# Sorting graph nodes on one core: destination blocks counted ahead of the weights, and row tiles mixed with the rank products

## What is computed

```python
edge_index = jnp.stack([src, dst])
x = x + _L0_gnn_ref(_layernorm(x), W, a_src, a_dst, edge_W, edge_b, bias, edge_attr_3, edge_index)
x = x + _L0_ffn_ref(_layernorm(x)[None], ...)[0]
x = x + _L1_gnn_ref(_layernorm(x), W_u, b_u, W_v, src, dst)
x = x + _L1_ffn_ref(_layernorm(x)[None], ...)[0]

# inside _L0_gnn_ref
h = (x @ W.T).reshape(n, H, D)
alpha = einsum(h[src], a_src) + einsum(h[dst], a_dst) + sum(enc * h[dst])   # then a softmax over each dst
out = jax.ops.segment_sum(h[src] * attn[..., None], dst, num_segments=n)
```

## Time and profile before

| | us |
|---|---|
| median of 3 runs | 4083.69 (4081.59 to 4086.49) |
| profiled execution, total | 4077.23 |
| its span | 4075.5 |
| sort stage, start to DVE's last operation | about 226 |
| last gather issued | 123.8 |
| ranks start on PE | 143.3 |
| placing starts on PE | 197.8 |

### The profile page before, as it was taken

One profiled execution on the slowest core, in us unless ns is written; L12 is line 12 of the kernel. 1 busy time (PEld: TensorE's weight loads), 2 busy tenths in 40 slices (PEclk: granted clock), 3 DMA queues, 4 the chain that ended last, 5 costly groups with the idle time before them and its releaser, 6 DMA issues. The chain is left out here.

```text
span 4075.5 us, 69197 instructions
## 1 busy us (share of the span) xinstructions
PE 2987.4 (73%) x12787; PEld 2165.0 (53%) x12788; DVE 2290.8 (56%) x5023; ACT 1295.0 (32%) x5485; POOL 2294.7 (56%) x2343
## 2 busy tenths in 40 slices
PE   4624777788888877989666656566665489999998
PEld 3422444444444444658544444444444388888887
DVE  4534888888888887864355555555555611111111
ACT  1402444444444444432211111111111533333333
POOL 5156777677777772002577777777777523333332
PEclk9857999899999998988777877877777799999999
DMA  8545444344444442000244444444444766665564
GB/s 185 152 92 131 114 115 113 100 106 105 105 105 105 108 108 53 0 2 32 78 112 113 113 113 113 113 112 113 113 113 112 216 186 168 166 170 165 170 174 123
DMA packets 284454, 477.32 MB, mean 117 GB/s; under 512 B 143854, under 2 KB 185660, under 8 KB 283892
## 3 DMA queue, kind: packets, MB, share of 16 engines
q0 software_dynamic: 127312, 321.61, 32.2%
q1 hardware_dynamic: 148203, 151.72, 12.7%
q10 hardware_dynamic: 8880, 3.34, 0.4%
HBM read 426.29 MB, written 50.68 MB: 117 GB/s over the span
## 5 line engine op out<-in xcount | busy, mean ns | idle before, releaser
L945 PE MATMUL g_pA<-g_msg,k_ident 128*128 128x264 f32 (+1 forms) x3712 | 1153.1, 464 | 475.5 <-DVE g_pA L1139 411.6
L945 PEld LDWEIGHTS g_pA<-g_msg,k_ident 128*128 128x128 f32 x3712 | 808.4, 229 | 808.7 <-issue 661.9
L900 POOL DMA_INDIRECT g_rows<-own,g_recs x928 | 879.4, 948 | 333.9 <-issue 262.8
L900 POOL DMA_INDIRECT g_rows<-rows,g_recs x928 | 879.6, 948 | 296.6 <-issue 194.7
L934 PE MATMUL g_pE<-g_ew,g_recT 128*128 128x512 f32 x932 | 515.4, 680 | 242.1 <-DVEq L1123 238.8
L1133 DVE TENSOR_TENSOR g_msg<-g_rows,g_pp 128x1024 f32 (+3 forms) x464 | 571.9, 1233 | 151.4 <-DVEq L84 151.3
L1983 POOL DMA_INDIRECT out<-e_ys,e_goal x102 | 160.6, 1575 | 505.8 <-issue 486.3
L934 PEld LDWEIGHTS g_pE<-g_ew,g_recT 128*128 128x128 f32 x932 | 171.4, 203 | 459.1 <-DVEq L1123 331.2
L2036 PE MATMUL e_pY<-e_w,e_hT 128*128 x1632 | 373.8, 382 | 35.5 <-issue 35.5
L1055 ACT ACTIVATE g_pp<-g_dd 128x32 f32<-128x32 f32 x464 | 95.2, 205 | 918.5 <-ACTq L84 918.5
L2025 PEld LDWEIGHTS e_pH<-e_xT,e_w 128*128 128x128 f32 x3264 | 381.6, 192 | 5.2
(11 more groups left out here) (419 smaller groups left out, 3533.5 us busy)
## 6 DMA issues: line engine op xcount, KB each, us to landing
e_w<-in_L_ffn_W SPq DMA_DIRECT2D x110, 1024.0 KB
g_rows<-own,g_recs POOLq DMA_INDIRECT x928
g_rows<-rows,g_recs POOLq DMA_INDIRECT x928
g_recs<-slots SPq DMA_DIRECT2D x468, 8.0 KB
tok<-e_xall SPq DMA_DIRECT2D x7, 910.0 KB
own<-p_row SPq DMA_DIRECT2D x50, 119.0 KB
p_x<-in_x SPq DMA_DIRECT2D x1, 5600.0 KB
own<-p_x SPq DMA_DIRECT2D x1, 5600.0 KB
```

What stands on the lines that cost most here:

```text
L900: pool.indirect_dma_start(out=rows[:, r, j, :], out_offset=None, in_=rows_d, in_offset=bass.IndirectOffsetOnAxis(ap=recs[:, r, 4 * j:4 * j ...
L945: last = t_.matmul(sums, K["ident"][:], of, start=False, stop=(j == C - 1), skip_group_check=True)
```

## The change

DVE's order is new: `index(0)` to `index(4)` and counts 0 to 19 first, then the record copies, counts 20 and 21, the weight preparation, and 50 statistics with a count after every third (counts 22 to 37); variance; count 38; scales; counts 39 to 49. On PE, 16 tiles come ahead of the ranks, two follow each of the seven rank steps, and 20 come last. POOL, ACT and SP keep their programs, UR = 3 included. `tiles` replaces `group`, and `ranks` becomes one step.

```diff
-        UR = 3
+        UR, EARLY = 3, 16
@@ VectorE
                 index(0)
-
+                index(1)
+                index(2)
+                for t in range(4):
+                    count(t)
+                index(3)
+                for t in range(4, 7):
+                    count(t)
+                index(4)
+                for t in range(7, 20):
+                    count(t)
+                dve.wait_ge(e_in, 64)
+                v.tensor_copy(rec[:, :, 0].bitcast(I32), srcw[:]).then_inc(rec_made, 1)
+                v.tensor_copy(rec[:, :, 1:4], attrw[:]).then_inc(rec_made, 1)
+                count(20)
+                count(21)
                 dve.wait_ge(w_in, 64)
...
                 dve.wait_ge(x_in, 32)
-                half = NT // 2
-                for t in range(half):
+                for t in range(NT):
                     norm.tile(v, t, x[:, t:t + 1, :])
-                for g in range(1, NT // GT):
-                    index(g)
-                for t in range(R):
-                    count(t)
-                for t in range(half, NT):
-                    norm.tile(v, t, x[:, t:t + 1, :])
+                    if t % 3 == 2:
+                        count(22 + t // 3)
                 ch.link(v.memset(norm.a[:], 0.0))
                 norm.variance(v, ch, stats)
-                dve.wait_ge(e_in, 64)
-                v.tensor_copy(rec[:, :, 0].bitcast(I32), srcw[:]).then_inc(rec_made, 1)
-                v.tensor_copy(rec[:, :, 1:4], attrw[:]).then_inc(rec_made, 1)
+                count(38)
                 dve.wait_ge(sq, 1)
                 norm.scales(v, ch, rst)
-                for t in range(R, NT):
+                for t in range(39, NT):
                     count(t)
@@ TensorE
-                def group(u, first, last_group):
-                    for r in range(W):
-                        if r < W - 1 or not last_group:
-                            turn(W * u + (r + 1), (r + 1) % 2)
-                        product(W * u + r, r % 2, first and r < 2)
+                def tiles(lo, hi):
+                    for t in range(lo, hi):
+                        if t + 1 < NT:
+                            turn(t + 1, (t + 1) % 2)
+                        product(t, t % 2, t < 2)
...
-                group(0, True, False)
-                group(1, False, False)
-                group(2, False, False)
-                ranks()
-                group(3, False, False)
-                group(4, False, True)
+                tiles(0, EARLY)
+                pe.wait_ge(hot_ok, 1)
+                for j in range(len(cols)):
+                    ranks(j)
+                    tiles(EARLY + 2 * j, EARLY + 2 * j + 2)
+                tiles(EARLY + 2 * len(cols), NT)
```

More of the change, by code:

```diff
@@ L536, in product, with ranks @@
                     last.then_inc(h_ok, 1)
-                def group(u, first, last_group):
-                    for r in range(W):
-                        if r < W - 1 or not last_group:
-                            turn(W * u + (r + 1), (r + 1) % 2)
-                        product(W * u + r, r % 2, first and r < 2)
[L544 to L552, removed]
+                def tiles(lo, hi):
[3 more added lines that the diff above has]
+                        product(t, t % 2, t < 2)
+                def ranks(j):
+                    a, b = cols[j]
+                    h = wide[:, a * NB:b * NB]
+                    w = (b - a) * NB
+                    if j:
+                        pe.wait_ge(taken, j)
+                    t_.matmul(pR[0:P, 0:w], K["tri"][0:P, 0:P], h, start=True, stop=True)
+                    t_.matmul(pTt[:, 0:w], K["ones"][0:P, 0:P], h, start=True, stop=True).then_inc(mm_ok, 1)
                 def place(g):
```

## The result

The changed kernel takes 4098.09 us (median; 4095.19 to 4100.98) where the kernel before takes 4083.15 beside it (4081.59 to 4086.49). The ratio is 1.0035, 95% interval 1.0023 to 1.0047: 14.9 us slower. 4090.5 was forecast, with a range up to 4097. Direction and mechanism were right; the loss is twice the forecast and 1 us beyond the range.

A forecast was written before the change was run, and what follows sets the result against it. The sort was taken as a chain hardly anything overlaps; the scan comes 14 earlier, but row tiles wait behind x's store, so placing starts 7.4 later, minus 0.6: +6.8, median 4090.5, range 4072 to 4097.

The forecast's parts named there:

- ACT's start: ACT's first row tile, after VectorE's counts and statistics: at 103.3 against 78.64, 24.7 later, with 1.3 added for slower landings.
- third rival: VectorE's statistics wait behind counts of late gathers: ACT up to 3.6 later, +10.4 in all, 4094; chance 0.12.
- catch up: VectorE's mixed loop, at 1.56 per count against POOL's 1.507, was said to recover from late gathers.
- PE's 16 tiles: TensorE's tiles ahead of the ranks: 25.2 from ACT's start, ending last, so ranks start at 128.5 against 143.25.
- The rank steps: TensorE's ranks mixed with tiles: 1.98 plus 2.5 for two tiles, period 4.5, 27.8 in all; scan at 156.9.
- x's issue: SP's store of x, still after row 29, now falls among row tiles: issued at 160.2, just as tiles 30 to 49 begin.
- Row 30's landing: Row 30's store, behind x in SP's queue and needed by row 35: lands 25 after 160.2, at 185.2; bounds 19 to 28.
- From there to placing: Fourteen tiles 18.6, low clock 2.2, minus 0.8: placing starts at 205.2, 7.4 later; tenth group 0.6 nearer.
- It costs nothing: SP's store of x in the kernel before, holding SP from 126.4 to 144.2 when no row tile runs, was priced at nothing.
- POOL: POOL's gathers: gather 13 leaves at 53.6, later ones every 1.507 without stall, the last at 107.9, 15.9 earlier.
- SP doesn't hold the tiles: Second x issue returns at once or row stores overtake x: placing 12.2 earlier, -12.8 in all, 4070.9; chance 0.14.
- short drain: Row 30 lands 19 after x's issue, the tail being mixed traffic's: +0.8, 4084.5; chance 0.14.

The follow-up runs named there:

- split runs: Changed kernel with x's 112 partitions stored after row 29 and its 13 after all rows: ratio 1.0016 to the kernel before; parts exchanged: 0.9990.
- x after row 39: Kernel before with UR = 4, so its store of x comes ten rows later: ratio 1.0030 to the kernel before, +13.3 us.

## Why the prediction was wrong in size

The sum to the placing was off by 6.3: +5.4 - 3.2 + 0.1 + 3.9 + 0.1.

- **ACT's start, +5.4: the failed step.** "Landings under it took up to 8.6 instead of 6.3; I add 1.3 (bounds 0 and 3.6)". One count waited 6.43 there, 5.1 more than that term. The statistics had begun 0.8 late (73.47 for 72.7), and the way from the last of them to ACT was 0.5 shorter, which makes the 5.4. The 8.6 was read from gathers issued from 80.07 on, when the record store had been in flight for two us and POOL had just paused. In the new order gathers are issued right at the store's start (71.75), and ten of them took 10.2 (median; up to 12.5). Moving the store away brought the landings back to 5.0 and removed the wait, so the cause is shown; that it is the first moments of the store that slow a gather most is my reading of two orders. It was the third rival's mechanism, and more than its 3.6: I gave it 0.12 as an alternative, and it came on top of my case. Nor did the loop "catch up", as I had it: from 82.53 on DVE has no pause in it (1.55 a round, as forecast), so it has no slack to make a wait good with.
- **PE's 16 tiles, 0.** Forecast 25.2 from ACT's start to the ranks; measured 133.93 - 108.70 = 25.2. The tiles ended last, as said.
- **The rank steps, -3.2.** Forecast period 4.5, measured 3.99 (133.93 to 137.92). I had 1.98 for the two rank products and 2.5 for two tiles, between PE's pace and ACT's. In the timeline they take 1.72 and 2.27; in the window PE is busy for all 3.99 and ACT for 2.42, so ACT no longer sets any of the pace.
- **x's issue, +0.1** from the scan (3.37 for 3.3). The step that the diff does not mention, and on which the forecast turned, was right: undoing it alone brings 20.6 us back (from +14.9 to -5.7).
- **Row 30's landing, +3.9: mis-sized.** Forecast 25 with bounds 19 and 28; measured 28.9, and 28.7 with `UR = 4`. I had the 27.2 of the drain from the row and went below it for the older traffic. The split runs show that the tail is x's own: the row store lies behind both parts, and the full drain is a lower bound, with the store's own time on top.
- **From there to placing,** 20.1 for 20.0, with two tiles at the granted clock of 0.53 (products of 2.03 and 1.70); the last group is 0.6 nearer, as said.
- **"It costs nothing"** of x's old place was wrong: DVE waited 7.16 for `following` beside it, and the ranks started about 6 later for it (x after row 39). It changed nothing in the sum, since the tiles ended last after the change (one-hot ready at 122.6, forecast 126.5).
- **POOL,** +2.3 on the last gather: gather 13 left at 54.87 instead of 53.6, and one issue took 2.09 instead of 1.20. The tiles hid it.

The rival that SP doesn't hold the tiles is refuted by the evictions. The short drain is too: it needed 19, and row 30 took 28.9, or 22.7 with the large part alone ahead of it. The range failed because its top put the bounds of my own case and the rival's delay side by side, not one on the other: the start's +5.4 and the landing's +3.9 make +9.3, and only the rank steps took 3.2 of it back. Each was beyond its own bound (+2.5 for the ranks' start, or 3.6 by the rival; 28 for the landing, which took 28.9). That the median passed 4097 hangs besides on the 2 us outside the stage: 4083.7 + 12.7 is 4096.4.

## What to carry to other kernels

Before you move compute, list the large stores of every queue and ask which wait each one stands ahead of in the new order. Five row buffers cover five tiles, 6.7 us here; a store that drains for 29 uncovers everything behind it. Moving such a store only pays if nothing that is read soon is in flight beside it: the record store was waited for in each of the three other places tried (6.43, 5.92, 5.12) and not behind the first 30 rows. And where two delays have independent causes, the range must take in their sum.

## What the runs showed of the hardware

- The 5600 KB part of x is accepted in 0.74 and the next DMA of SP's queue is held: a row store for 14.5, the small part of x for 15.4 to 17.0. Behind the small part alone one row store was held, for 4.19.
- The 13-partition part of x drains for some 8 us by itself, most of them at 70 to 76 GB/s, where the 112-partition part moves at some 300.
- x issued on POOL's queue holds POOL for 2.90 and still slows the row stores on SP's: they hold SP for 1.1 to 4.5 each instead of 0.31, and seven evictions wait, 19.0 in all.
- Indirect gathers of 425 elements by 125 partitions take 5.0 on their own and 10.2 (up to 12.5) when issued with a 1.66 MB store.
- DVE waits 1.75 to 2.44 for a DMA of 0.5 KB with x out of the way, and 7.16 with x in flight.
